# One-hots of edge moves, destinations and histogram laid out in pairs of columns instead of eight, ten or twenty-four

## What is computed

```python
h = (x_flat @ W_gat).reshape(M, HEADS, NUM_EXPERTS)
src = concat([edge_index[0], loops]); dst = concat([edge_index[1], loops])
e = leaky_relu(a_src[src] + a_dst[dst])
ee = exp(e - segment_max(e, dst)[dst])
denom = segment_sum(ee, dst)
agg = segment_sum(h[src] * (ee / denom[dst])[:, :, None], dst) + b_gat
scores = _layernorm(agg).reshape(M, HEADS, NUM_EXPERTS).mean(1)
```

## Time and profile before

| what | value |
|---|---|
| time, median of 3 runs | 966.31 us (965.25 to 967.83) |
| time of the profiled execution | 966.39 us |
| span of the profiled execution | 964.6 us |
| mean granted TensorE clock | 0.674 of full speed |
| TensorE matmul busy | 655.8 us (68%) |
| VectorE busy | 570.8 us (59%) |
| GpSimd busy | 330.9 us (34%) |
| ScalarE busy | 272.9 us (28%) |

### The profile page before, as it was taken

One profiled execution on the slowest core, in us unless ns is written; L12 is line 12 of the kernel. 1 busy time (PEld: TensorE's weight loads), 2 busy tenths in 40 slices (PEclk: granted clock), 3 DMA queues, 4 the chain that ended last, 5 costly groups with the idle time before them and its releaser, 6 DMA issues. The chain is left out here.

```text
span 964.6 us, 12524 instructions
## 1 busy us (share of the span) xinstructions
PE 655.8 (68%) x4227; PEld 399.3 (41%) x4227; DVE 570.8 (59%) x1281; ACT 272.9 (28%) x520; POOL 330.9 (34%) x384
## 2 busy tenths in 40 slices
PE   6338688679999958307557345450967872889996
PEld 5214355346556637103223223220865551733442
DVE  6967999998542467387655445637451438294222
ACT  1033222112111323013322122321024334345553
POOL 6013132122111312457777477740002110122332
PEclk9995555555555655558575677765556995589999
DMA  5000000000000000501212112100000000000000
GB/s 177 1 1 1 1 1 1 1 1 1 1 1 1 2 2 0 79 6 35 36 22 35 18 22 35 22 6 0 1 0 1 1 1 1 0 1 12 11 11 11
DMA packets 26728, 13.42 MB, mean 14 GB/s; under 512 B 20435, under 2 KB 23860, under 8 KB 26422
## 3 DMA queue, kind: packets, MB, share of 16 engines
q1 hardware_dynamic: 21430, 11.08, 4.5%
q0 software_dynamic: 5248, 1.68, 2.4%
HBM read 11.19 MB, written 1.55 MB: 13 GB/s over the span
## 5 line engine op out<-in xcount | busy, mean ns | idle before, releaser
L1398 POOL DMA_INDIRECT edge_src_row<-src_rows_dram,slot_src_index x160 | 173.6, 1085 | 59.1 <-issue 48.0
L568 POOL TENSOR_TENSOR wa_scores<-wa_scores,wa_max 128x512 f32<-128x512 f32 x32 | 35.3, 1103 | 164.1 <-DVE wa_max L749 164.1
L466 POOL TENSOR_TENSOR ln_xs<-xn,ln_stats 128x256 f32<-128x256 f32 x32 | 21.0, 666 | 156.1 <-DVE ln_stats L439 92.4
L613 PE MATMUL wa_s_ps<-wa_kbd,wa_qk 64*64 64x512 f32 x128 | 61.3, 1054 | 15.2 <-issue 15.2
L512 PE MATMUL ln_pT<-ident,ln_xs 128*64 128x128 f32 x128 | 30.8, 410 | 50.2 <-POOL ln_xs L466 49.5
L1813 PE MATMUL moe_h_ps<-xT,moe_w 128*128 (+1 forms) x128 | 63.2, 630 | 1.7 <-ACTq L1895 1.7
L1504 PE MATMUL edge_acc<-edge_scratch 128*32 128x128 bf16 x672 | 44.4, 410 | 22.7 <-DVE edge_scratch L1279 22.7
L706 ACT ACTIVATE wa_probsT<-wa_t_ps 128x512 f32<-128x512 f32 x32 | 19.1, 597 | 140.9 <-PE wa_t_ps L621 140.9
L1910 DVE SCALAR_TENSOR_TENSOR moe_weighted<-moe_y_ps,moe_b_cols,moe_G 128x512 f32<-128x512 f32 x32 | 22.6, 746 | 61.1 <-ACT moe_G L1892 60.7
L1485 PE MATMUL edge_both<-dst_table,edge_onehot_T 128*128 128x24 bf16 x160 | 6.7, 180 | 69.4 <-DVE values_from_edges L1268 59.0
L562 POOL TENSOR_TENSOR wa_kbd<-wa_qk,headmask 128x512 f32<-128x512 f32 x32 | 34.1, 1067 | 46.0 <-ACT wa_qk L683 46.0
(11 more groups left out here) (379 smaller groups left out, 1474.7 us busy)
## 6 DMA issues: line engine op xcount, KB each, us to landing
edge_onehot_T<-slot_lo_dram SPq DMA_DIRECT2D x16, 320.0 KB, 3.6
edge_src_row<-src_rows_dram,slot_src_index POOLq DMA_INDIRECT x160, 2.4
edge_scratch<-in_L_ffn_edge_index SPq DMA_DIRECT2D x2, 1024.0 KB, 5.8
xrow<-in_x SPq DMA_DIRECT2D x4, 256.0 KB, 7.7
out_h<-h SPq DMA_DIRECT2D x4, 256.0 KB, 2.6
moe_w<-in_L_ffn_W SPq DMA_DIRECT2D x2, 256.0 KB
src_rows_dram<-src_rows SPq DMA_DIRECT2D x1, 320.0 KB
moe_w<-in_L_ffn_W SPq DMA_DIRECT2D x2, 128.0 KB
```

The costliest lines, as they stand in the source:

```text
L568: pool.tensor_tensor(sc[b][:], sc[b][:], bc(mx[b][:], WIN), ALU.subtract).then_inc(shifted, 1)
L613: ins = pe.matmul(s_ps[b][half], qk[b][half, 0, :], kbd[b][half])
L1398: pool.indirect_dma_start(gs[b][:, j, :], None, srow_dram, bass.IndirectOffsetOnAxis(edges.src_index[:, x:x + 1], axis=0))\
```

## The change

In every one-hot the columns of a chunk lie in pairs: the layout is (pair of columns, count, 2) instead of (count, columns of the chunk). Column i of a chunk is then at [i // 2, :, i % 2], and its elements are 2 elements (4 bytes) apart. The table of comparison holds each number twice (128 x 2) whatever the chunk, and is repeated over the pairs by the access pattern. The values are repeated along the count two at a time. `iota_rep` shrinks from 1280 to 256 elements, and one table `iota_twice` of 256 elements, made by one instruction, takes the place of `iota_lo16` and `iota_hi16`. The numbers of elements of all one-hots, the number of their instructions, the order of the work and all waits but that on the tables (3 becomes 2) are as before.

```diff
+def equal(eng, out, index, values):
+    pairs, n = out.shape[1], out.shape[2]
+    return eng.tensor_tensor(out, bc_at(index[:, 0:n], 1, pairs),
+                             bc_at(values.rearrange("p (c x) -> p c x", x=2), 2, n), ALU.is_equal)
+
+def weighted_by(eng, out, onehot, values):
+    return eng.tensor_tensor(out, onehot, bc_at(values.rearrange("p (c x) -> p c x", x=2), 2, out.shape[2]), ALU.mult)
...
-        self.iota_rep = mem.sb("iota_fp16_repeated", [P, P, RCH], F16)
+        self.iota_rep = mem.sb("iota_fp16_twice", [P, P, 2], F16)
...
-        self.onehot = mem.sb("slot_onehot", [P, RCHUNKS, P, RCH], BF16)
+        self.onehot = mem.sb("slot_onehot", [P, RCHUNKS, PER, P, 2], BF16)
...
-        pool.tensor_copy(self.iota_rep[:], bc(self.iota16[:], RCH)).then_inc(self.filled, 1)
+        pool.tensor_copy(self.iota_rep[:], bc(self.iota16[:], 2)).then_inc(self.filled, 1)
...
-            dve.tensor_tensor(row, rep, bc_at(row16[:, part], 1, P), ALU.is_equal).then_inc(self.move_ready, 1)
-            at = self.at_col[:, 0:wide]
-            self.after(dve, dve.tensor_tensor(at, rep[:, 0:wide], bc_at(col16[:, part], 1, wide), ALU.is_equal))
-            dve.tensor_tensor(col[:, 0, 0:wide], at, bc_at(high16[:, part], 1, wide), ALU.mult)\
-               .then_inc(self.move_ready, 1)
-            self.after(dve, dve.tensor_tensor(col[:, 1, 0:wide], at, bc_at(low16[:, part], 1, wide), ALU.mult))
+            row, col, at = self.to_row[j % RING], self.to_col[j % RING], self.at_col[:, :, 0:wide]
+            equal(dve, row, iota, row16[:, part]).then_inc(self.move_ready, 1)
+            self.after(dve, equal(dve, at, iota, col16[:, part]))
+            weighted_by(dve, col[:, 0, :, 0:wide], at, high16[:, part]).then_inc(self.move_ready, 1)
+            self.after(dve, weighted_by(dve, col[:, 1, :, 0:wide], at, low16[:, part]))
...
-            dve.tensor_tensor(self.onehot[:, c], self.iota_rep[:], bc_at(part, 1, P), ALU.is_equal)\
-               .then_inc(self.onehot_ready, 1)
+            equal(dve, self.onehot[:, c], self.iota_rep[:], part).then_inc(self.onehot_ready, 1)
...
-                    ins = pe.matmul(slots[:, :, PER * low:PER * high], self.to_row[j % RING][:, :, i],
-                                    self.to_col[j % RING][:, :, 0:PER * (high - low), i], start=False,
+                    ins = pe.matmul(slots[:, :, PER * low:PER * high], self.to_row[j % RING][:, i // 2, :, i % 2],
+                                    self.to_col[j % RING][:, :, i // 2, 0:PER * (high - low), i % 2], start=False,
...
-                dve.tensor_tensor(clo[q], iota_lo16, bc_at(edges.last_lo[:, part], 1, P),
-                                  ALU.is_equal).then_inc(clo_ready, 1)
-                dve.tensor_tensor(chi[q], iota_hi16, bc_at(edges.last_hi[:, part], 1, TILES),
-                                  ALU.is_equal).then_inc(chi_ready, 1)
+                equal(dve, clo[q], iota_twice, edges.last_lo[:, part]).then_inc(clo_ready, 1)
+                equal(dve, chi[q], iota_twice, edges.last_hi[:, part]).then_inc(chi_ready, 1)
...
-            dve.tensor_copy(iota_lo16, bc(iota16[:], CCH)).then_inc(iota_ready, 1)
-            dve.tensor_copy(iota_hi16, bc(iota16[:, 0:TILES], CCH)).then_inc(iota_ready, 1)
+            dve.tensor_copy(iota_twice, bc(iota16[:], 2)).then_inc(iota_ready, 1)
...
-                                    edges.onehot[:, c, :, j], parts[b][:, j].rearrange("p s v -> p (s v)"),
+                                    edges.onehot[:, c, j // 2, :, j % 2], parts[b][:, j].rearrange("p s v -> p (s v)"),
...
-                    ins = pe.matmul(count_acc[g:g + TILES], chi[q][:, :, j], clo[q][:, :, j], start=False, stop=False,
+                    ins = pe.matmul(count_acc[g:g + TILES], chi[q][:, j // 2, :, j % 2], clo[q][:, j // 2, :, j % 2], start=False, stop=False,
```

More of the change, by code:

```diff
@@ L841, in stage @@
         self.slot = [room[:, x * RC:(x + 1) * RC].bitcast(I32) for x in range(8, 10)]
-        room = self.onehot[:].rearrange("p c q j -> p (c q j)")
+        room = self.onehot[:].rearrange("p c i q j -> p (c i q j)")
         self.match = room[:, 0:TILES * SPAN].rearrange("p (t c) -> p t c", t=TILES)
         row, col = GCH * P, GCH * 2 * REACH * PER
-        self.to_row = [room[:, b * row:(b + 1) * row].bitcast(F16).rearrange("p (q c) -> p q c", c=GCH)
+        self.to_row = [room[:, b * row:(b + 1) * row].bitcast(F16).rearrange("p (c q x) -> p c q x", c=GCH // 2, x=2)
                        for b in range(RING)]
         room = room[:, RING * row:]
-        self.to_col = [room[:, b * col:(b + 1) * col].bitcast(F16).rearrange("p (x q c) -> p x q c", c=GCH, x=2)
-                       for b in range(RING)]
+        self.to_col = [room[:, b * col:(b + 1) * col].bitcast(F16)\
+                       .rearrange("p (y c q x) -> p y c q x", y=2, c=GCH // 2, x=2) for b in range(RING)]
         room = room[:, RING * col:]
-        self.at_col = room[:, 0:col // 2].bitcast(F16).rearrange("p (q c) -> p q c", c=GCH)
+        self.at_col = room[:, 0:col // 2].bitcast(F16).rearrange("p (c q x) -> p c q x", c=GCH // 2, x=2)
         room = room[:, col // 2:]
@@ L1005, in form @@
                 dve.wait_ge(self.moved, j - RING + 1)
-            part, rep = slice(GCH * j, GCH * j + GCH), self.iota_rep[:, :, 0:GCH]
-            row, col = self.to_row[j % RING], self.to_col[j % RING]
-            dve.tensor_tensor(row, rep, bc_at(row16[:, part], 1, P), ALU.is_equal).then_inc(self.move_ready, 1)
-            at = self.at_col[:, 0:wide]
-            self.after(dve, dve.tensor_tensor(at, rep[:, 0:wide], bc_at(col16[:, part], 1, wide), ALU.is_equal))
-            dve.tensor_tensor(col[:, 0, 0:wide], at, bc_at(high16[:, part], 1, wide), ALU.mult)\
-               .then_inc(self.move_ready, 1)
-            self.after(dve, dve.tensor_tensor(col[:, 1, 0:wide], at, bc_at(low16[:, part], 1, wide), ALU.mult))
+            part, iota = slice(GCH * j, GCH * j + GCH), self.iota_rep[:]
+            row, col, at = self.to_row[j % RING], self.to_col[j % RING], self.at_col[:, :, 0:wide]
[3 more added lines that the diff above has]
+            self.after(dve, weighted_by(dve, col[:, 1, :, 0:wide], at, low16[:, part]))
             dve.sem_inc(self.move_ready, 1)
@@ L1173, in graph_router @@
     wide, narrow = P * CCH, TILES * CCH
-    clo = [room[:, b * wide:(b + 1) * wide].rearrange("p (q c) -> p q c", c=CCH) for b in range(2)]
-    iota_lo16 = room[:, 2 * wide:3 * wide].rearrange("p (q c) -> p q c", c=CCH)
+    clo = [room[:, b * wide:(b + 1) * wide].rearrange("p (c q x) -> p c q x", c=CCH // 2, x=2) for b in range(2)]
     room = room[:, 3 * wide:]
-    chi = [room[:, b * narrow:(b + 1) * narrow].rearrange("p (q c) -> p q c", c=CCH) for b in range(2)]
-    iota_hi16 = room[:, 2 * narrow:3 * narrow].rearrange("p (q c) -> p q c", c=CCH)
+    chi = [room[:, b * narrow:(b + 1) * narrow].rearrange("p (c q x) -> p c q x", c=CCH // 2, x=2) for b in range(2)]
+    iota_twice = room[:, 2 * narrow:2 * narrow + 2 * P].rearrange("p (q x) -> p q x", x=2)
     lo_row = [loop.sb(f"edge_onehot_T{b}", [P, RCH * P], BF16) for b in range(2)]
@@ L1369, in _ @@
                                         bc(from_last[:, :, hh, GE], GE), ALU.mult))
-            dve.wait_ge(iota_ready, 3)
+            dve.wait_ge(iota_ready, 2)
             for c in range(RCHUNKS):
@@ L1559, in graph_router @@
     loop.__exit__()
-    room = edges.onehot[:].rearrange("p c q j -> p (c q j)").bitcast(F32)
+    room = edges.onehot[:].rearrange("p c i q j -> p (c i q j)").bitcast(F32)
     agg, nrm, sq = (room[:, x * TILES * W:(x + 1) * TILES * W].rearrange("p (t f) -> p t f", f=W) for x in range(3))
```

## The result

| what | before | after |
|---|---|---|
| time, median | 965.78 us (4 runs, 962.67 to 967.83) | 924.27 us (4 runs, 922.85 to 925.10) |
| ratio, 95% interval | | 0.9569 (0.9542 to 0.9596) |
| span of the profiled execution | 964.6 us | 923.0 us |
| mean granted TensorE clock | 0.674 | 0.676 |
| TensorE matmul busy | 655.8 us | 602.1 us |

The change takes 41.5 us off by the medians and 41.6 us off by the spans, where 23.1 us had been forecast: 924 us against 943, and outside the range (929 to 952).

A forecast was written before the change was run, and what follows sets the result against it. TensorE, full at 1.2 GHz in the window attention with its strided moves, was taken as the bound there; 17.5 + 3.6 + 1.8 + 0.2 = 23.1 us off 966.39 gave 943 us, range 929 to 952.

The forecast's parts named there:

- the sum: Gains added: 17.5 seven steps, 3.6 early steps, 1.8 tables, 0.2 one-hot weights; 23.1 us off, to 943 us.
- The rival that the columns stay as slow: Moves on TensorE: columns stay at 1.78 ns because something other than the step is slow; 964 us, chance 0.05.
- the slower rival: Pair runs cost VectorE's one-hots their double rate: 993 us, or 977 us in a milder form; chance 0.11 for both.
- the milder form: VectorE's one-hots: a repeating word makes the data part 1.69 times as long; 977 us, or 975 by the skill page.
- The wait ahead of the loop: GpSimd's idle time before a gather, ended by VectorE's chain: one table copy instead of two takes off 1.8 us.
- The histogram's shorter matmuls: Counts in the router's loop get shorter on a TensorE that waits anyway, hidden by GpSimd's gathers; no gain counted.
- VectorE's cover in the wide steps: Widest steps with moves: VectorE needs 8.4 us, TensorE up to 9.2, leaving 0.8 us before VectorE sets the step.
- the choice that the clock stays at 0.50: Main case: TensorE's granted clock stays at 1.2 GHz in the steps with moves; 943 us, chance 0.50.
- the rival, with its mechanism: Unstalled columns raise TensorE's clock in the steps with moves: 929 us throughout, 935 us for part; chance 0.30.
- the seven steps: Window attention steps with moves, 239.65 to 317.30 us, TensorE full; 18,640 columns at 0.84 instead of 1.78 ns gain 17.5 us.
- The two that were priced: Steps at 217.71 to 239.65 us, only half bound by TensorE; gain 3.6 us, with bounds 0 and 4.5.
- The one ahead of them: The step ahead of the two early steps, taken as still more VectorE's; no gain counted.

The follow-up runs named there:

- e2: Changed kernel with only the moves' weights back in runs of eight, 16 bytes apart, moving operand in pairs; 952.87 us, ratio 0.9613 to the kernel before.
- e3: Changed kernel with only the moves' moving operand back in runs of eight, 16 bytes apart, weights in pairs; 988.68 us, ratio 1.0012 to the kernel before.
- e1: Changed kernel with the moves' weights and moving operand both back in runs of eight, 16 bytes apart; 990.22 us, ratio 0.998 to the kernel before.
- e5: Changed kernel with the moves' one-hots in runs of four, columns 8 bytes apart; 924.44 us, ratio 0.9574 to the kernel before.
- e6: Changed kernel with the moves' one-hots in single columns, 2 bytes apart, values repeated one by one; 956.79 us, ratio 0.9897 to the kernel before.
- e9: Changed kernel with the first of a step's two moves put ahead of the scores on TensorE; 953.41 us, ratio 0.9641 to the kernel before.
- e10: Changed kernel with both of a step's moves put ahead of the scores on TensorE; 951.67 us, ratio 0.963 to the kernel before.
- e12: Changed kernel with both moves ahead of the scores and one VectorE product in place of two per chunk; 949.49 us, ratio 0.9581 to the kernel before.
- e8: Kernel before with 32 zero-weight unstrided matmuls added in one run behind the scores of each step with moves; 988.98 us, ratio 1.0247 to the kernel before.
- e7: Changed kernel with one of each chunk's eight move matmuls, the other seven left out; 930.02 us, ratio 0.9636 to the kernel before.

## Why the prediction was wrong

**Right: the mechanism, and the column at half clock.** 16 bytes cost 1.79 ns and 4 bytes 0.84 at 0.50, as the sum had them, and by e2 and e3 it is the moving operand's step, not the weights'. e1 confines nearly all of the gain to the moves. The rival that the columns stay as slow is refuted by the same rows. The rule of the Trainium skill that was cited (SBUF — State Buffer, Door 1: The DMA port swizzle: a 16-byte line must be hit twice to read at full rate) made 16 bytes slow and 4 free, and agrees with that; but 8 bytes, two hits a line, take 0.90 ns at the full clock (e5) against 0.47 to 0.50 for 4, so at the full clock this kernel's operand wants more than two hits.

**Right: VectorE's instructions.** 1749 for 1750 ns, and the slower rival is refuted for pairs at both its prices; the gathers stay at 1082 ns. The double rate is lost where a single 16-bit element repeats (e6, 1220 ns). The page of the Trainium skill that was cited for the milder form (Vector Engine (DVE) Microarchitecture Reference, Measured stream behaviour on trn2) gave 975 us if its rule for single words held for a word that stays in place; these rows don't show it there.

**Right: tables and cover.** The wait ahead of the loop fell by 1.95 us for 1.8 forecast. The histogram's shorter matmuls gave nothing, as costed. The 0.8 us of VectorE's cover in the wide steps was gone, and what was late next is what had been named, VectorE with its two moves a step: in four of the wide steps it is busy 30.30 of 32.01 us.

**Wrong: the choice that the clock stays at 0.50.** The text had the rival, with its mechanism (full as TensorE was, half its cycles streamed nothing) and its price (14 us in the seven steps), and gave it 0.30 against 0.50. What spoke against it, "6.35 us steps just as full stay at 0.50", was no evidence: those steps hold no moves, so they say nothing about steps in which fp16 columns stream without a stall behind the scores. With the moving columns at 16 bytes these steps stayed at 0.50 (before, e1, e3), with 4 or 8 bytes the mean rose to 0.82 to 0.90 (changed kernel, e2, e5; with another order of work 0.69 in e9 and 0.86 in e10). In the seven steps the clock gave an estimated 11.1 us (28.6 against 17.5; with the clock at 0.50 throughout they would have taken 44.45 + 18,640 x 0.84 ns = 60.1 us, and took 49.06).

**Wrong: where the rival's effect was thought to end.** Its price was bounded by the seven steps, and 929 us was taken as the end of the range. But the steps behind the moves, up to the last transpose, are 4.0 us shorter in all (4.08 for 6.35, 4.75 for 5.98, 6.48 for 4.26, 4.34 for 6.95), at a mean clock of 0.81 instead of 0.63. The text had counted nothing there. Part of this is luck: in e12, at 0.59, the same stretch takes 38.95 us, as long as before.

**Mis-sized: the early steps.** The two that were priced gave 4.0 us (17.95 for 21.94) against 3.6. The one ahead of them, for which nothing was counted as being still more VectorE's, gave 1.1 us (10.37 for 11.50) with the clock at 0.50 before and after: its shorter columns were not hidden. With all this and the small terms below, the end of the range should have been some 922.

**Small terms.** The shorter copy of `iota_rep` on GpSimd was costed at nothing. The first transpose comes 0.8 us sooner, 86.60 for 87.37; the kernels here without a table of eight or ten had 85.7 to 86.8 there, and those with one 86.9 to 87.8. That fits, but the two ranges nearly touch, and it was not tried by itself. The loop and all behind it gained 1.0 for 0.2 forecast. The wait ahead of the loop, with the stretch before it, gave 2.1 for 1.8. In all 11.1 (clock in the seven steps) + 1.5 (early steps) + 4.0 (behind the moves) + 0.8 + 0.3 + 0.8 = 18.5 us beyond the sum, which is 41.6 - 23.1.

**Open.** Why the clock falls back in single steps of the changed kernel (at 219, 236, 253 and 266 us) and in others not is not settled. Order alone (e9, e10) moves these places without a pattern that one trace each can show, and the clock differs where nothing was changed: the step from about 130 us, long before the moves, takes 6.36 and 6.35 us at 0.50 in the kernels before and after, and 4.70 us at 1.00 in e12.

## What to carry to other kernels

A stalled matmul can cost twice: its own time, and the clock that TensorE is granted when its columns stream steadily, for itself and for the fp32 work around it. Here the seven steps lost 17.5 us of the first and some 11 of the second. Where a fix turns stalled columns into steady ones and the profile shows the low clock on a full TensorE, cost the stage at both levels, up to the engine that comes next, and let the range reach past the stage's end, where the clock may or may not stay up. And lay a one-hot out so that both readers get what they want: for the 16-bit moving operand 4 bytes between columns, for VectorE a repeated pair instead of a repeated single element.

## What the runs showed that was not expected

- The time of a moving column 8 or 16 bytes from the last doesn't depend on the clock: 1.79 ns for 16 bytes at 0.50 and at 1.00 (before and e8), 0.91 and 0.90 ns for 8 bytes (e5). For 4 bytes it is 0.84 and 0.47 to 0.50 ns.
- Taking away seven eighths of the moves' matmuls (e7) made the kernel no faster: its seven steps have a clock of 0.63 and take 50.85 us, with the moves 0.86 and 49.06.
- Ten runs of 32 steady matmuls would take 10 x 32 x 128 x 0.84 ns = 34 us at half clock; in e8 they cost 2.47% of the kernel before, 24 us. Each run raises the clock, and it is lost again in or behind the 16-byte moves that follow.
- The histogram's matmuls, 48 bytes apart before, take 1.51 us for 24 of 128 columns (482.58 to 484.09 us), 0.49 ns a column, against 0.76 us and 0.25 ns after (441.65 to 442.41 us), both at a clock of 0.50: far less than 16 bytes cost in the moves. They go to four groups of 32 output partitions in turn; whether that is why was not tried.
